# The low parts of the experts' weights in a decoder layer: all twelve on VectorE instead of seven on GpSimd and five on VectorE

## What is computed

```python
def _moe(x, gate, w1, w2, w3):          # 4 experts, top 2, 256 -> 768 -> 256
    xf = x.reshape(-1, D)
    probs = jax.nn.softmax(xf @ gate, axis=-1)
    w, idx = jax.lax.top_k(probs, TOP_K)
    w = w / jnp.sum(w, axis=-1, keepdims=True)
    oh = jax.nn.one_hot(idx, N_EXPERTS, dtype=xf.dtype)
    comb = jnp.einsum('nk,nke->ne', w, oh)
    for e in range(N_EXPERTS):
        h = jax.nn.silu(xf @ w1[e]) * (xf @ w3[e])
        out = out + comb[:, e:e + 1] * (h @ w2[e])
```

## Time and profile before

| | us |
|---|---|
| median of 3 runs | 1502.42 |
| lowest and highest | 1502.37, 1502.48 |
| the profiled execution | 1502.61 |
| its span | 1500.7 |
| TensorE matmul busy | 1225.5 (82%) |
| VectorE busy | 1008.9 (67%) |
| ScalarE busy | 638.3 (43%) |
| GpSimd busy | 265.4 (18%) |

### The profile page before, as it was taken

The page is one execution under the profiler, slowest core; times in us unless marked ns, Lnnn a source line. Parts: engine busy times, 40 slices in busy tenths (PEclk is TensorE's granted clock), DMA queues, the critical chain, the costliest instruction groups (busy, mean ns, idle before and its releaser), DMA issues. The chain is left out here.

```text
span 1500.7 us, 24288 instructions
## 1 busy us (share of the span) xinstructions
PE 1225.5 (82%) x7994; PEld 1086.0 (72%) x7994; DVE 1008.9 (67%) x3074; ACT 638.3 (43%) x1370; POOL 265.4 (18%) x199
## 2 busy tenths in 40 slices
PE   1679987968799697779996968799787149999997
PEld 1467986946689696567996946689687148888886
DVE  6875766668477666785766668567667875555553
ACT  4325635733266175324644723256265403333331
POOL 2200003311000150100003301000141612333332
PEclk9889997988899888789997987899889559999999
DMA  6005510010164001004510010064330001222221
GB/s 231 1 1 123 136 38 1 2 56 1 42 145 96 15 1 42 15 1 113 134 36 15 1 57 1 22 154 106 143 125 10 21 14 25 40 36 36 37 41 23
DMA packets 45256, 80.32 MB, mean 54 GB/s; under 512 B 8432, under 2 KB 18160, under 8 KB 44496
## 3 DMA queue, kind: packets, MB, share of 16 engines
q1 hardware_dynamic: 36976, 69.19, 17.1%
q0 software_dynamic: 6720, 9.18, 3.8%
q10 hardware_dynamic: 1440, 0.39, 0.1%
HBM read 28.01 MB, written 8.78 MB: 25 GB/s over the span
## 5 line engine op out<-in xcount | busy, mean ns | idle before, releaser
L921 ACT ACTIVATE b_pp<-b_pp,b_nm 128x256 f32<-128x256 f32 x256 | 116.0, 501 | 86.9 <-DVE b_nm L959 86.0
L800 PEld LDWEIGHTS bank<-b_va,b_pt 128*128 128x128 f32 x1024 | 127.6, 191 | 4.0
L800 PE MATMUL bank<-b_va,b_pt 128*128 128x65 f32 x1024 | 128.5, 269 | 0.0
L1187 PE MATMUL bank<-c_kv,c_qv 128*128 128x128 f32 (+1 forms) x512 | 95.5, 316 | 7.3 <-ACT c_kv L1302 7.3
L1209 PE MATMUL bank<-c_v,c_pt 128*128 128x68 f32 x768 | 101.1, 268 | 0.1
L1145 POOL TENSOR_SCALAR c_qv<-c_rot,const 128x512 fp32r<-128x512 f32 x56 | 86.8, 1567 | 77.9 <-ACT c_rot L1298 77.9
L1209 PEld LDWEIGHTS bank<-c_v,c_pt 128*128 128x128 f32 x768 | 97.9, 192 | 1.7 <-DVE c_pt L1409 0.7
L959 DVE CUSTOM_DVE_ANT_0 b_pp<-bank,mask 128x256 f32<-128x256 f32 x256 | 97.0, 418 | 0.0
L100 PE MATMUL bank<-e_up_low,e_xh 128*128 x210 | 89.7, 427 | 1.8 <-DVE e_xl L178 1.8
L1401 DVE CUSTOM_DVE_ANT_0 c_pp<-bank,const 128x128 f32<-128x128 f32 (+1 forms) x256 | 80.2, 351 | 10.0 <-PE bank L1187 10.0
L1568 POOL DMA_INDIRECT out<-e_ys,e_ids x35 | 55.5, 1586 | 164.2 <-DVE e_ys L1803 160.4
(11 more groups left out here) (368 smaller groups left out, 3631.2 us busy)
## 6 DMA issues: line engine op xcount, KB each, us to landing
b_kst<-b_kh SPq DMA_DIRECT2D x128, 128.0 KB, 2.3
k_low_twice<-b_kl SPq DMA_DIRECT2D x128, 128.0 KB, 2.4
b_qst<-b_ql SPq DMA_DIRECT2D x64, 128.0 KB, 2.3
raw_up<-in_w SPq DMA_DIRECT2D x4, 768.0 KB, 10.3
raw_down<-in_w SPq DMA_DIRECT2D x4, 768.0 KB, 12.1
XN<-in_x SPq DMA_DIRECT2D x5, 512.0 KB, 3.4
context<-in_ctxT SPq DMA_DIRECT2D x4, 512.0 KB, 4.7
mask<-in_mask SPq DMA_DIRECT2D x4, 512.0 KB, 5.6
```

What stands on the lines that cost most here:

```text
L800: ins = pe.matmul(O2[u % 2][:, at:at + VW], pt[:, n % 2, kt * S + qt * P:kt * S + (qt + 1) * P], va[:, b * QT + kt, 2 * j + hp, :], start= ...
L921: act.activation(pp[:, n % 3, qt, :], pp[:, n % 3, qt, :], ACT.Exp, bias=nm[:, n % 4, qt:qt + 1], scale=-1.0).then_inc(s["probs_exp"], 1)
L1187: ins = pe.matmul(SB[n % 3][:, qt * P:qt * P + w], qv[:, m % 2, r, at:at + P], kv[:, m % 2, part, b * S:b * S + w], start=part == 0, stop= ...
```

## The change

`BY_VECTOR` and `BY_POOL` go. GpSimd's stream starts with the wait for `slots_ready`. VectorE makes pieces 0 to 3 behind line 1722, ahead of its wait for `counted`, and pieces 4 to 11 where its five stood. TensorE waits for one semaphore, `weights_low`, instead of two.

```diff
--- before.py
+++ after.py
@@ -1526,9 +1526,6 @@
         END = HID - MID
         gathered = [s[f"gathered_{i}"] for i in range(3)]
         PIECES = [(0, e, k) for e in range(NE) for k in range(KD)] + [(1, e, 0) for e in range(NE)]
-        BY_VECTOR = (1, 4, 6, 9, 11)
-        BY_POOL = [i for i in range(len(PIECES)) if i not in BY_VECTOR]
-
         def piece(ws_, i):
             part, e, k = PIECES[i]
             return ws_[1][:, e].rearrange("p a b -> p (a b)") if part else ws_[0][:, e, k]
@@ -1545,11 +1542,6 @@
 
         @block.gpsimd
         def _(pool):
-            for n, i in enumerate(BY_POOL):
-                pool.wait_ge(s["weights_high"], i + 1)
-                pool.tensor_tensor(piece(wl, i), piece(RAW, i), piece(wh, i).bitcast(F32),
-                                   ALU.subtract).then_inc(s["weights_low_by_pool"], 1)
-
             def gather(n):
                 if n >= 3:
                     pool.wait_ge(s["x_turned"], n - 2)
@@ -1623,8 +1615,7 @@
                 ins.then_inc(s["down_ready"], 1)
 
             pe.wait_ge(s["slots_ready"], 1)
-            pe.wait_ge(s["weights_low_by_pool"], len(BY_POOL))
-            pe.wait_ge(s["weights_low_by_vector"], len(BY_VECTOR))
+            pe.wait_ge(s["weights_low"], len(PIECES))
             turn_x(0)
             expert = [None] * 2
             for n in range(SLOTS + 1):
@@ -1688,11 +1679,10 @@
         def _(dve):
             ch = Chain(dve, s["chain"])
 
-            def low_piece(j):
-                i = BY_VECTOR[j]
+            def low_piece(i):
                 dve.wait_ge(s["weights_high"], i + 1)
                 dve.tensor_tensor(piece(wl, i), piece(RAW, i), piece(wh, i).bitcast(F32),
-                                  ALU.subtract).then_inc(s["weights_low_by_vector"], 1)
+                                  ALU.subtract).then_inc(s["weights_low"], 1)
 
             for r in run:
                 ch.then(dve.memset(r[:, 0:PAD], 0.0))
@@ -1720,6 +1710,8 @@
             leftb = left.unsqueeze(2).to_broadcast([P, NT, NE])
             ch.link(dve.tensor_tensor(off[:], sel[:], leftb, ALU.mult))
             ch.then(dve.scalar_tensor_tensor(out=off[:], in0=leftb, scalar=-1.0, in1=off[:], op0=ALU.add, op1=ALU.subtract))
+            for i in range(4):
+                low_piece(i)
             dve.wait_ge(s["counted"], 1)
             sums = SUMS[:, 0:2 * NT * NE].rearrange("p (c t e) -> p c t e", c=2, e=NE)
             ch.link(dve.tensor_copy(run[0][:, PAD:], sums[:, 1]))
@@ -1766,8 +1758,8 @@
                                                  op0=ALU.is_ge, op1=ALU.add))
             ch.then(dve.tensor_copy(which[:], whichf[:]))
             ch.then(dve.tensor_scalar(past[:], numbers, begin[:, NE:NE + 1], tok[:, 0:1], ALU.is_ge, ALU.mult))
-            for j in range(len(BY_VECTOR)):
-                low_piece(j)
+            for i in range(4, len(PIECES)):
+                low_piece(i)
             dve.wait_ge(s["lists_ready"], NE)
             ch.link(dve.tensor_copy(ws[:], LIST[:, SW:2 * SW]))
             ch.then(dve.tensor_tensor(ws[:], ws[:], LIST[:, 2 * SW:3 * SW], ALU.add))
@@ -1838,7 +1830,7 @@
          "k_turned k_copied next_normed next_low next_turned heads_turned heads_low out_projected h_normed "
          "h_turned y_high qk_rotated next_high heads_high h_ready h_squares h_high chain layer_norm_ready")
 SEM_E = ("tables_in logits_ready logits_copied logits_shifted gate_exp chain chosen counted weights_rounded "
-         "positions_ready lists_ready slots_ready weights_high weights_low_by_pool weights_low_by_vector "
+         "positions_ready lists_ready slots_ready weights_high weights_low "
          "gathered_0 gathered_1 gathered_2 x_turned x_high x_low up_first up_last up_mid first_tanh last_tanh "
          "first_silu last_silu last_ready first_ready hidden_turned hidden_high hidden_low down_ready rows_scaled scattered")
```

## The result

The changed kernel takes 1493.97 us (median of 6 runs, 1493.41 to 1494.91) against 1502.45 us for the kernel before (median of 6, 1502.09 to 1504.98): a ratio of 0.9939 with a 95% interval of 0.9926 to 0.9952, or 8.5 us less where 9.5 were forecast. The profiled execution took 1494.91 us with a span of 1493.1.

The account below looks back on a forecast made before the run. The prediction took VectorE's chain from the choice of experts to the first gather as the bound. Stalls removed, work added and clock, -20.8 + 11.7 - 0.4 = -9.5 us, gave 1492.9 us, range 1491.8 to 1494.8.

Parts of the forecast that it names:

- VectorE's chain bounds the stretch: From the choice of experts to the first gather, every microsecond VectorE gains or loses reaches the end one to one.
- Stalls that go: Lines 1712 to 1729: seven VectorE operations each sat out one GpSimd instruction; removing those saves 20.8 us.
- Added work: Seven more pieces on VectorE's chain at 1.67 us each add 11.7 us, at most 12.3.
- Early pieces: The four pieces behind line 1722 don't wait for ScalarE's rounding; the first starts near 1172.9 us; cost nothing.
- the rival that priced them at GpSimd's 3.41 us: Early pieces run slow beside ScalarE's rounding, giving back 7.0 us, 1499.9 us in all; 3 in 100.
- The lists: The last expert's list matmuls stay covered by 13.4 us of late pieces; without cover some 2.5 us would show.
- Clock: TensorE's low clock level at the experts' start shortens from 5.3 to 4.35 us, gaining 0.4, bounds 0.9 and nothing.
- The sum: All terms together, -20.8 + 11.7 - 0.4 = -9.5 us, taken from the median of 1502.42 us, forecast 1492.9 us.

Follow-up runs that it names:

- down_late_b: The changed kernel with the four down-weight pieces off the chain, two behind the identifiers, two behind the first rows' low part; 1489.55 us.
- by_bank_b: The changed kernel with all low parts behind the identifiers: first bank's columns for all experts, the other two banks', then the down pieces; 1489.98 us.
- pool_writes: The kernel before with GpSimd's seven subtractions replaced by seven memsets of the same tiles, which read nothing; 1485.49 us.
- pool_at_lists: The kernel before with GpSimd's seven subtractions starting only when the first expert's marks are done; 1504.11 us.
- repeats: The kernel before with seven more 1536-element subtractions on VectorE behind its five, GpSimd keeping its seven; 1515.24 us.
- after_again: The changed kernel measured again, unaltered, beside variants on one chip; 1494.62 us.
- third_bank_late: The changed kernel with only the first 1024 columns of each up piece on the chain, the third bank's columns and the down pieces later; 1485.15 us.
- the two repeats: The changed kernel measured twice more, unaltered, each time beside variants on the same chip; 1494.62 and 1494.69 us.
- down_later: The changed kernel with the four down-weight pieces off the chain and none started until the first gather has landed; 1487.09 us.

## Why the prediction was right

- *VectorE's chain bounds the stretch.* Shown: seven more pieces lengthen the whole by 12.4 us, and in every variant but two the stretch shrinks and grows with VectorE's chain alone; in `down_late_b` and `by_bank_b` the first gather's longer instruction comes on top.
- *Stalls that go, -20.8 us.* In the changed kernel the nine operations take 1182.32 - 1174.02 - 6.67 = 1.63 us up to the copy and 1183.22 - 1182.80 = 0.42 for the two additions (in the chain), 2.05 together, against 22.82 before: 20.8 us. That GpSimd's subtractions cause them is shown by `pool_writes` (they go with the subtractions) and `pool_at_lists` (they move with them).
- *Added work, +11.7 us.* Pieces follow at 1.67 us (6.67 for four, in the early block and in the late ones): 7 x 1.67 = 11.7. `repeats` measured 11.4 on the stretch and 11.68 in its rows. The prediction's upper bound of 12.3 us has each piece start only after the 1.75 us of the one before; the pieces start 1.67 us apart, so a piece begins 0.08 us before the last has ended. That bound is also what the first half of the sentence from the Trainium skill (VectorE: DVE Perf Modes, section "The DRAIN you can't avoid") would give; the rows side with its second half.
- *Early pieces.* 1.67 us each beside ScalarE as without; the rival that priced them at GpSimd's 3.41 us falls. The first began at 1.63 us behind the choice, as forecast (1172.9 against 1171.33).
- *The lists.* The last one's matmuls ran under the late pieces, no wait. `by_bank_b`, which has no piece there, waited 2.41 us (the prediction's 2.5).
- *Clock, -0.4 us.* Low for 4.2 us instead of 5.3: (5.3 - 4.2) x 0.45 = 0.5 us. The size fits, but it isn't shown that the change made it. The changed kernel has 4.1 to 4.2 us in three profiles, `repeats` and `pool_at_lists`, with GpSimd's subtractions in place, 4.2 and 3.6, `down_late_b` without them 5.9. This term came out by luck.
- *The sum.* The stretch gave -9.11 us where its terms said -9.1, and the rest -1.18: 0.5 of it is the clock, and most of what is left the last scatter's landing, 3.87 us where it was 4.61, which belongs to no step of the change. That would be 10.3 us, and two executions in which the choice starts alike show it: 1502.61 us before (1171.33) and 1492.34 in `after_again` (1171.52). The medians differ by less, 8.5, 8.2 and 9.1 us on three occasions, probably because they mix executions with early and late starts; only the profiled ones show theirs. What was off is the base. I took the terms from 1502.42 us, the median of three runs within 0.1 us of each other, while more runs of the same kernel go from 1502.07 to 1505.78, and the profiled execution had the earliest start of the choice that I saw (1171.33, once more in `third_bank_late`; the others up to 1174.55). So the kernel's own runs are 3.7 us wide, wider than the whole stated range of 3.0 us. The mechanism and both large terms are right; that the median fell inside the range is in part luck: the two repeats gave 1494.62 and 1494.69, 0.1 to 0.2 us below its upper end of 1494.8.

## What to carry to other kernels

Before giving elementwise work to GpSimd to relieve VectorE, look at VectorE's small operations beside it: if there is one long row for each GpSimd instruction, the helper costs nearly its own full length on VectorE's chain, here 3.0 us of its 3.4, for 1.67 us of relief. Then ask what of the work the next step needs at all: the larger gain here (7.6 to 9.5 us more) came from making late what is needed late. But what is made late must not leave TensorE waiting in the loop: in `by_bank_b` 11.2 of the 15.4 us gained ahead of it were lost again in it, part of that because the clock fell during a wait. And judge a step of a few microseconds by the stretch around it in the trace, since the start of that stretch may wander by more than a term of the sum.

## What I had not expected of the hardware

- VectorE's subtraction holds up the gather's instruction on GpSimd: 2.62 us (`down_late_b`) instead of 1.19 (`down_later`), with only VectorE's pieces moved away from it. Beside two subtractions of 2048 elements it took 3.15 us (`by_bank_b`). VectorE's operations there have two SBUF inputs; other kinds were not tried beside a gather.
- A memset on GpSimd holds a tensor_scalar on VectorE (0.66 and 0.88 us instead of 0.20 and 0.16) and not additions with two inputs. A scaled copy on GpSimd holds conversions and tensor_scalars of 4 to 64 elements up to its end, one of them for 4.0 us, and two-input operations up to 0.8 us before its end.
- The wait is mutual: beside VectorE's long operations GpSimd's subtraction of 3.4 us is 4.2 to 4.7 us long.
